# Delta rule on one core: the order tables of TensorE, ScalarE, VectorE and GpSimd written anew

## The reference, cut to what matters

```
q, k, v = silu(conv4(h @ W));  q, k = rotary(q), rotary(k);  beta, gamma = sigmoid(h @ Wb), sigmoid(h @ Wgamma)
q, k = l2norm(q), l2norm(k);  v = v * beta;  kb = k * beta;  gm = mean over each chunk of gamma
A = -(kb @ k.T) * strict_lower;  for i in 1..31: A[i, :i] += A[i, :i] @ A[:i, :i];  T = A + I
u = T @ v;  w = T @ kb
for each chunk:  attn = q @ k.T * tril;  u_t = u - w @ S;  o = q @ S + attn @ u_t;  S = g * S + k.T @ u_t
x1 = x + rmsnorm(fractal_mixer(h)) * gate + (rmsnorm(o) @ Wo)
```

## Time and profile before

| | |
|---|---|
| median of three runs | 2488.2 us |
| the profiled execution's own time | 2490.37 us |
| its span (first to last instruction) | 2488.6 us |
| granted TensorE clock over the span | 0.983 of full speed |
| busy over the span: TensorE, VectorE, GpSimd, ScalarE | 94%, 70%, 54%, 50% |
| busy from 1035 to 1648 us: the same four | 587.9, 461.8, 327.2, 291.7 us of 613 |

### The profile page before, as it was taken

The page is one execution under the profiler, slowest core; times in us unless marked ns, Lnnn a source line. Parts: engine busy times, 40 slices in busy tenths (PEclk is TensorE's granted clock), DMA queues, the critical chain, the costliest instruction groups (busy, mean ns, idle before and its releaser), DMA issues. The chain is left out here.

```text
span 2488.6 us, 56588 instructions
## 1 busy us (share of the span) xinstructions
...
## 2 busy tenths in 40 slices
...
DMA packets 192530, 122.10 MB, mean 49 GB/s; under 512 B 87728, under 2 KB 170672, under 8 KB 192256
## 3 DMA queue, kind: packets, MB, share of 16 engines
...
## 5 line engine op out<-in xcount | busy, mean ns | idle before, releaser
L1615 POOL TENSOR_TENSOR m_hid_part<-m_hid,m_hid_part 128x512 fp32r<-128x512 f32 x176 | 238.1, 1353 | 553.8 <-ACT m_hid_part L1524 550.5
L991 POOL TENSOR_TENSOR a_bm<-a_bias,a_mask_add 128x512 f32<-128x512 f32 (+3 forms) x512 | 438.2, 877 | 119.9 <-DVE a_nm L726 113.9
L902 ACT ACTIVATE a_S<-a_S,a_nm 128x512 f32<-128x512 f32 (+3 forms) x512 | 289.6, 566 | 231.6 <-DVE a_nm L726 226.9
L726 DVE CUSTOM_DVE_ANT_0 a_S<-a_S,a_bm,a_nsn 128x512 f32<-128x512 f32 (+3 forms) x512 | 276.4, 546 | 78.2 <-PE a_S L476 69.3
L1536 ACT ACTIVATE m_hid<-m_G 128x512 f32<-128x512 f32 x176 | 105.5, 599 | 390.1 <-PE m_G L1470 355.8
L476 PE MATMUL a_S<-a_kT,a_qT 128*128 128x384 f32 (+3 forms) x1024 | 284.6, 361 | 0.7 <-DVE a_nm L726 0.5
L1697 DVE TENSOR_TENSOR m_hid<-m_hid,m_U 128x512 f32<-128x512 f32 x176 | 121.1, 688 | 223.2 <-PE m_U L1470 189.6
L1487 PE MATMUL m_Y<-m_hid_part,m_down_high 128*128 128x512 f32 x704 | 256.5, 405 | 12.3 <-POOL m_hid_part L1615 11.5
L1470 PE MATMUL m_G<-m_in,m_gate_high 128*128 128x512 f32 x704 | 251.8, 398 | 0.9 <-POOL m_up_low L1609 0.9
L1470 PE MATMUL m_U<-m_in,m_up_high 128*128 128x512 f32 x704 | 250.7, 396 | 1.5 <-DVE m_hid L1697 1.2
L486 PE MATMUL a_T<-s_ident,a_S 128*128 128x128 f32 x1280 | 230.2, 278 | 19.4 <-ACT a_PT L911 15.4
...
## 6 DMA issues: line engine op xcount, KB each, us to landing
a_o<-s_weight_rows SPq DMA_DIRECT2D x128, 128.0 KB, 3.0
...
m_spread<-s_w ACTq DMA_DIRECT2D x128, 128.0 KB, 2.9
...
```

Source lines behind the costliest of these rows:

```text
L726: dve.tensor_tensor_reduce(S[:, n % S_SLOTS, 0:w], SB[n % 2][:, 0:w], bm[:, n % BM_SLOTS, 0:w], -1.0, nsn[:, tile % 2, h:h + 1], ALU.add, ...
L902: act.activation(S[:, n % S_SLOTS, 0:w], S[:, n % S_SLOTS, 0:w], ACT.Exp, scale=-1.0, bias=nm[:, tile % 2, h:h + 1], accum_out=den[:, tile ...
L991: pool.tensor_tensor(bm[:, n % BM_SLOTS, 0:w], bias[:, h, L - w:L], mask_add[b % 2][:, 0:w], ALU.add).then_inc(s["bm_ready"], 1)
L1615: pool.tensor_tensor(hid_part[1][:, q % H_SLOTS], hid[:, q % G_SLOTS], hid_part[0][:, q % H_SLOTS].bitcast(F32), ALU.subtract).then_inc(hi ...
```

## The change

Only the four tables are written in another order. Every piece is still there, once per round and with the same lag, so each engine issues the same operations on the same data; semaphores, tiles and DMAs are the same. Of the diff a few lines are enough:

```diff
-            ("ocopy", 0, K), ("ocopy", 1, K), ("M", 1, R), ("silu", 0, IN), ("silu", 1, IN), ("proj", 4, IN),
...
+            ("silu", 0, IN), ("ocopy", 0, K), ("ocopy", 1, K), ("M", 1, R), ("silu", 1, IN), ("osq", 0, K),
...
-            ("S", 12, R), ("attn", 2, F), ("low", 1, IN), ("attn", 3, F), ("xg", 0, F),
...
+            ("S", 12, R), ("attn", 2, F), ("attn", 3, F), ("xg", 0, F), ("low", 1, IN), ("S", 13, R), ("vb", 0, IN),
...
-            ("kb", 0, F), ("gxm", 0, F), ("ors", 0, K), ("rot", 0, IN), ("rot", 1, IN), ("nb", 0, IN), ("rrn", 0, IN),
...
+            ("gxm", 0, F), ("nb", 0, IN), ("kb", 0, F), ("ors", 0, K), ("rot", 0, IN), ("rot", 1, IN),
+            ("rot", 2, IN), ("rrn", 0, IN), ("rrn", 1, IN), ("rot", 3, IN), ("rrn", 2, IN), ("rrn", 3, IN),
```

More of the change, by code:

```diff
@@ L1922, in delta_phase @@
         PE_ROUND = [
[L1923 to L1938, removed]
-        ACT_ROUND = [
-            ("ocopy", 0, K), ("ocopy", 1, K), ("M", 1, R), ("silu", 0, IN), ("silu", 1, IN), ("proj", 4, IN),
[L1941 to L1952, removed]
@@ L1953, in delta_phase @@
-        DVE_ROUND = [
[L1954 to L1965, removed]
-            ("S", 12, R), ("attn", 2, F), ("low", 1, IN), ("attn", 3, F), ("xg", 0, F),
-            ("S", 13, R), ("vb", 0, IN), ("conv", 0, NX), ("xg", 1, F),
-            ("S", 14, R), ("vb", 1, IN), ("conv", 1, NX), ("xg", 2, F), ("gates", 0, NX), ("xg", 3, F)]
+            ("qp", 0, R), ("M", 1, R), ("step", 0, R), ("fast", 0, R), ("proj", 4, IN), ("au", 0, R), ("step", 1, R),
@@ new lines, in delta_phase @@
+            ("mixer", 2, F), ("mixer", 3, F), ("core", 0, K), ("uw", 0, F), ("qkT", 0, IN), ("step", 7, R),
+            ("fast", 7, R), ("au", 3, R), ("step", 8, R), ("fast", 8, R), ("attn", 0, F), ("step", 9, R),
+            ("fast", 9, R), ("uw", 1, F), ("uw", 2, F), ("core", 1, K), ("step", 10, R), ("fast", 10, R),
+            ("qkT", 1, IN), ("qkT", 2, IN), ("attn", 1, F), ("uw", 3, F), ("qkT", 3, IN), ("step", 11, R),
+            ("fast", 11, R), ("proj", 0, NX), ("gram", 0, IN), ("attn", 2, F), ("attn", 3, F), ("step", 12, R),
@@ new lines, in delta_phase @@
+            ("fast", 12, R), ("gram", 1, IN), ("gm", 0, F), ("v", 0, IN), ("step", 13, R), ("fast", 13, R),
+            ("proj", 1, NX), ("step", 14, R), ("fast", 14, R), ("gates", 0, NX), ("step", 15, R), ("fast", 15, R),
+            ("rest", 0, NX), ("v", 1, IN), ("proj", 2, NX), ("proj", 3, NX)]
+        ACT_ROUND = [
+            ("silu", 0, IN), ("ocopy", 0, K), ("ocopy", 1, K), ("M", 1, R), ("silu", 1, IN), ("osq", 0, K),
+            ("silu", 2, IN), ("proj", 4, IN), ("M", 2, R), ("M", 3, R), ("frac", 0, F), ("silu", 3, IN),
+            ("proj", 5, IN), ("z", 0, IN), ("M", 0, R), ("frac", 1, F), ("z", 1, IN), ("z", 2, IN), ("silu", 4, IN),
+            ("rsq", 0, IN), ("onT", 0, K), ("rsq", 1, IN), ("z", 3, IN), ("onT", 1, K), ("rsq", 2, IN),
+            ("frac", 2, F), ("qkT", 0, IN), ("frac", 3, F), ("hs", 0, NX), ("rsq", 3, IN), ("uw", 0, F),
+            ("uw", 1, F), ("tap", 0, IN), ("uw", 2, F), ("tap", 1, IN), ("qkT", 1, IN), ("qkT", 2, IN),
+            ("qkT", 3, IN), ("silu", 5, IN), ("uw", 3, F), ("proj", 0, NX), ("gm", 0, F), ("proj", 1, NX),
+            ("proj", 2, NX), ("proj", 3, NX), ("gates", 0, NX)]
```

18 lines of the change are left out of this document (16 added, 2 removed).

## The result

The changed kernel takes 2530.9 us in the median of four runs (2526.5 to 2545.1), the one before 2487.8 us. The ratio is 1.0178, with a 95% interval of 1.0155 to 1.0200: 43 us slower, where 21 us slower were forecast, with a range that ended at 2522. The direction held, the size did not.

A forecast was written before the change was run, and what follows sets the result against it. A 66.2 us loop from inversion to inversion through GpSimd and VectorE bounds the late full rounds; 1.66 + 0.60 + 0.93 us make it 69.4. Over 6.5 loops 20.7 us, so 2509 us in the median, eight-in-ten range 2489 to 2522.

The forecast's parts named there:

- The loop already sets the length of the last full rounds.: Delta rule: a 66.2 us loop from inversion to inversion through GpSimd and VectorE, not TensorE's work, sets these rounds.
- Seven loops, the first by half: 20.7 us.: Batch elements 0 to 1 up to 6 to 7: 6.5 x 3.19 us added to the profiled time.
- `nb`, 1.66 us a loop, 11 us in all.: GpSimd: `nb` now stands between the inversion and `ors`, adding 1.66 us a loop, bounds 0.5 and 1.66.
- `low` 1, 1.53 us a loop, 10 us.: VectorE, late in the round: `attn` 3 and `xg` 0 now precede `low` 1, adding 1.53 to 2.16 us.
- `au` 0 waits 2.1 us for `ocopy`.: Start of a round: `silu` 0 and its table load precede `ocopy` on ScalarE, so TensorE waits 2.1 us.
- While the loop rules, this wait only takes the place of the waits for S further on, and I add nothing; bounds 0 and 1.9 us.: TensorE's wait before `au` 0 replaces later waits for S: nothing added, bounds 0 and 1.9 us.
- its last rival: TensorE waits of 2 us and more could drop its clock to 1.2 GHz; 0.14 together with both adding up.
- Both add up: TensorE's 1.9 us at `au` 0 enters the loop: 5.1 us x 6.5, 2521 us; 0.14 together with a falling clock.
- `T1` ahead of `on` costs nothing.: VectorE: `T1` waits some 7.2 us behind the inversion, `ors` ends 8.6 us behind it, so `on` loses nothing.
- The rest of the reordering, with a balance near nothing.: Other moves on VectorE, GpSimd and TensorE cancel, are hidden or give the loop nothing; the sum counts nothing for them.
- "Faster": VectorE's queue from `rotb` 0 to `rss` 1 shortens the loop by 1.5 us: 2480 us; chance 0.13.
- "no change": The order does nothing visible, gains and losses cancel: 2488 us, chance 0.06; within 0.2% in all 0.07.

The follow-up runs named there:

- Three moves on it: Kernel before with one move each: `nb` ahead of `kb` 2500.7 us; `low` 1 behind `attn` 3 and `xg` 0 2499.8 us; `low` 1 ahead of `mix` 1 2483.4 us.
- the wait before `au` 0 filled: Changed kernel with eleven unread products ahead of `proj` 4 on TensorE, all orders as changed: 2509.0 us.
- the run with nothing moved: Kernel before with eleven unread products ahead of `proj` 4 on TensorE, no order changed: 2494.1 us.
- all three moves taken back: Changed kernel with `silu` 0, `nb` (with `gxm`) and `low` 1 back in their old places, all other moves kept: 2499.7 us.
- the three moves: Kernel before with only `silu` 0, `nb` (with `gxm`) and `low` 1 moved as in the change: 2520.6 us.

## Why the forecast was right about the loop and wrong in its size

- **"The loop already sets the length of the last full rounds."** Right. Three moves on it, two of them longer and one shorter, each went the forecast way, and with the wait before `au` 0 filled, five loops of the changed kernel in a row are 69.2 to 69.8 us for the 69.4 of the sum.
- **Seven loops, the first by half: 20.7 us.** The total is near, the parts are not. Between the eight inversions, the kernel before takes 59.4, 63.0, 66.7, 66.1, 66.2, 66.5 and 62.3 us, the changed one with the wait filled 60.7, 69.7, 69.5, 69.6, 69.8, 69.2 and 63.3. The four loops in the middle grew by 3.2 us in mean, as forecast, the first and the last by about 1 and the second by 6.7. That the sum, 21.7 us, meets the forecast is luck in part.
- **`nb`, 1.66 us a loop, 11 us in all.** 14 us alone. The two loops grew by 1.5 and 2.5 us. Right, a little small.
- **`low` 1, 1.53 us a loop, 10 us.** 13 us alone; the two loops grew by 1.5 and 1.8 us. Right.
- **`au` 0 waits 2.1 us for `ocopy`.** Right: 2.12 us.
- **"While the loop rules, this wait only takes the place of the waits for S further on, and I add nothing; bounds 0 and 1.9 us."** This is the step that failed, and with it the sum. Its bounds counted the wait by its length. Behind the wait TensorE's clock was down for 6.8 us and more in every round that has it, the products under it took up to twice as long, `S` 2 came 3.0 us later by that in the round shown, and in four rounds of five GpSimd waited for `oss`, up to 4.7 us: 22 us in all on the changed kernel, shown by filling the wait with work. The forecast had the mechanism, as its last rival, without a place or a price, and put it in the upper end of the range with a share of 0.14 together with another case. The place was known: a wait of 2 us at one spot in every round. It should have been a term.
- **"Both add up" (2521 us).** Its time was the nearest to what came, but that is luck: its reason, that the lateness of `au` 0 enters the loop, is not the main one. That lateness costs 4 us, 9 at most, by the run with nothing moved. What the forecast held against it, that GpSimd knows nothing of `au`, was wrong too: `ors` waits for `oss`, and `oss` stands behind `S` 2.
- **`T1` ahead of `on` costs nothing.** Right for the total. The wait that the forecast did not expect is there once the clock stays up, 1.6 to 4.0 us in five rounds with the wait before `au` 0 filled. In one of these, from 1355.29 us on, it cost nothing, much as the forecast's 8.6 against 7.2 us implied: `on` begins 0.04 us behind the end of `ors`. With all three moves taken back `on` begins 1.8 us behind it (the lines above), and even so the total did not move when `T1` went back.
- **The rest of the reordering, with a balance near nothing.** Wrong by 12 us where it stands alone, 10 us (2530.9 less 2520.6) on top of the three moves. Neither `T1` nor `rrn` 0 holds it, the clock may have a part, and its cause stays open.
- **"Faster" and "no change"** are excluded by the interval.

Of the two rules of the Trainium skill that were weighed, one is measured. The drain of 1.38 us that the Trainium skill (ScalarE: Activation LUTs, "What ACT_TABLE_LOAD costs") adds to a table load is not in this trace: `silu` 0 starts 0.02 us behind its load of 1.28 us, and the wait before `au` 0 comes out at 2.12 us without it. The other, that of the ports which VectorE and GpSimd share (the Trainium skill, SBUF — State Buffer, "SBUF: two separate sides"), would have made `nb`'s move 0.5 us a loop cheaper than 1.66; the loops grew by 1.5 and 2.5 us, so nothing of that gain is seen, though no run here tests the rule by itself.
